# GpSimd writes the first two blocks' one-hots, and three more chunks are gathered raw

## What is computed

```
agg = segment_sum(layernorm(x)[src], dst)        # 106250 edges, 6250 nodes of 256 numbers
h   = relu(agg @ W_rel + b_rel + layernorm(x) @ W_root)
gates = h @ W_ih.T + b_ih + b_hh ; ... ; x = x + h_lstm @ W_fc + b_fc
x = x + ffn(layernorm(x))                        # slice softmax, attention over 64 slices per head
```

## Time and profile before

| | |
|---|---|
| median of 3 runs | 1261.83 us (1261.62 to 1261.88) |
| profiled execution, span | 1262.5 us |
| PE / PE weight load busy | 89% / 77% |
| DVE / ACT / POOL busy | 66% / 50% / 64% |

### The profile page before, as it was taken

How to read it: one execution, slowest core, us unless ns; L and a number is a source line. 1 busy time by engine, 2 the same in 40 slices (tenths; PEclk the granted TensorE clock), 3 DMA queues, 4 the chain that set the end, 5 groups by cost and what they waited for, 6 DMA issues and landing times. The chain is left out here.

```text
span 1262.5 us, 26644 instructions
## 1 busy us (share of the span) xinstructions
PE 1122.5 (89%) x9821; PEld 978.2 (77%) x9821; DVE 832.7 (66%) x2580; ACT 627.7 (50%) x1257; POOL 807.2 (64%) x850
## 2 busy tenths in 40 slices
PE   1058799999899999999999999999998999999998
PEld 1047688788788887888878787878787888897798
DVE  7885476567466765676667656775665667646665
ACT  5862344454455444544554545454543564545332
POOL 5277777777777777777777777777777777400000
PEclk9997999999899999999999999999998999999999
DMA  9573444444444444444444444444443444323398
GB/s 326 202 259 117 130 124 127 146 137 137 121 147 137 136 123 145 137 138 122 146 146 129 121 146 144 134 118 146 145 136 114 146 145 130 91 68 98 126 334 296
DMA packets 89761, 188.47 MB, mean 149 GB/s; under 512 B 19196, under 2 KB 51938, under 8 KB 89648
## 3 DMA queue, kind: packets, MB, share of 16 engines
q0 software_dynamic: 39888, 108.97, 29.9%
q1 hardware_dynamic: 38900, 57.91, 14.0%
q10 hardware_dynamic: 10859, 20.05, 4.5%
HBM read 154.86 MB, written 32.00 MB: 148 GB/s over the span
## 5 line engine op out<-in xcount | busy, mean ns | idle before, releaser
L618 POOL DMA_INDIRECT ring<-table,sidx x813 | 781.1, 961 | 271.6 <-issue 269.2
L397 PE MATMUL ps<-h_h,wih_h 128*128 128x250 f32 x1200 | 341.5, 285 | 0.0
L398 PE MATMUL ps<-h_l,wih_h 128*128 128x250 f32 x1200 | 338.8, 282 | 0.0
L399 PE MATMUL ps<-h_h,wih_l 128*128 128x250 f32 x1200 | 338.7, 282 | 0.0
L397 PEld LDWEIGHTS ps<-h_h,wih_h 128*128 128x128 f32 x1200 | 233.0, 194 | 1.6 <-issue 0.4
L398 PEld LDWEIGHTS ps<-h_l,wih_h 128*128 128x128 f32 x1200 | 232.8, 194 | 1.1
L399 PEld LDWEIGHTS ps<-h_h,wih_l 128*128 128x128 f32 x1200 | 232.5, 194 | 0.0
L983 PE MATMUL ps<-ring,oneh 128*32 128x512 f16 x2321 | 148.5, 386 | 55.1 <-DMA ring<-table,sidx 44.3
L762 ACT ACTIVATE gate<-ps,bgate 128x250 f32<-128x250 f32 x300 | 124.4, 468 | 143.1 <-PE ps L399 143.1
L1410 DVE TENSOR_SCALAR oneh<-iota,didx 128x64 f16<-128x64 f16 (+2 forms) x1199 | 183.2, 257 | 0.9 <-issue 0.9
L983 PEld LDWEIGHTS ps<-ring,oneh 128*32 128x32 f16 x2321 | 61.7, 97 | 125.0 <-DMA ring<-table,sidx 58.8
(11 more groups left out here) (211 smaller groups left out, 2480.1 us busy)
## 6 DMA issues: line engine op xcount, KB each, us to landing
ring<-table,sidx POOLq DMA_INDIRECT x813
swt_d<-swt ACTq DMA_DIRECT2D x25, 500.0 KB
gate<-swt_d SPq DMA_DIRECT2D x19, 500.0 KB, 5.9
x_room<-in_x SPq DMA_DIRECT2D x12, 512.0 KB, 10.2
xn<-table SPq DMA_DIRECT2D x25, 224.0 KB
xin<-in_x SPq DMA_DIRECT2D x25, 224.0 KB
res<-xin SPq DMA_DIRECT2D x25, 224.0 KB
table<-tile_room SPq DMA_DIRECT2D x8, 512.0 KB, 3.0
```

What stands on the lines that cost most here:

```text
L397: eng.matmul(dst, wh, xh, start=first, stop=False)
L398: eng.matmul(dst, wh, xl, start=False, stop=False)
L399: return eng.matmul(dst, wl, xh, start=False, stop=last)
L618: pool.indirect_dma_start(ring[:, j, :], None, table, bass.IndirectOffsetOnAxis(ap=idx, axis=0)).then_inc(done, 16)
```

## The change

1. POOL writes the one-hots of blocks 0 and 1 (`hots(pool, 0)`, `hots(pool, 1)`), after its raw gathers and before its wait for the stored table. DVE writes them only in the general branch; its turn 0 loses them.
2. `RAW` goes from 18 to 21, so `NE` from 6 to 7: 21 chunks are gathered raw and 810 from the table, and one more piece of three chunks is normalised in the ring.
3. The temporaries of all pieces lie in `norm_room`; the two lent table tiles begin at slot 21.
4. PE waits for all the raw pieces ahead of block 0's sums, where before it waited for each piece at its first use.

```diff
-    RAW = 18
+    RAW = 21
...
-        ln = [free[:, k * words:(k + 1) * words].rearrange("p (r c) -> p r c", c=C) for k in range(2)]
+        ln = [norm_room[:, k, :].rearrange("p (r c) -> p r c", c=C) for k in range(2)]
         tiles = [tile_room[:, k, :] for k in range(4)]
-        tiles += [free[:, (2 + k) * words:(3 + k) * words] for k in range(2)]
+        tiles += [free[:, k * words:(k + 1) * words] for k in range(2)]
...
-        e_ln = [norm_room[:, q, 0:3 * C].rearrange("p (r c) -> p r c", c=C) for q in range(2)]
 
         def ln_tmp(k):
-            return ln[k % 2] if k <= NCH else e_ln[k % 2]
+            return ln[k % 2][:, 0:ln_shape(k)[1], :]
...
+        def hots(eng, b):
+
+            e, (plan, _) = b % 2, hot_plan(b)
+            after(eng, sum_done[e], b // 2)
+            for j, (w0, w1, at) in plan.items():
+                n = WIN * (w1 - w0)
+                last = eng.tensor_scalar(oneh[:, e, at:at + n], iota[:, WIN * w0:WIN * w1], didx[:, j:j + 1],
+                                         -float(WN * b), ALU.subtract, ALU.is_equal)
+            last.then_inc(hot_done[e], 1)
...
             general = pool.value_load(flag_i[0:1, 0:1], min_val=0, max_val=1)
-            for q in range(TILES):
-                pool.wait_ge(ln_out[q], 16 * len(range(q, NCH + 1, TILES)))
-            pool.sem_inc(gather_go, 1)
+            pool.wait_ge(list_d, 2)
+
+            def table_stored():
+                for q in range(TILES):
+                    pool.wait_ge(ln_out[q], 16 * len(range(q, NCH + 1, TILES)))
+                pool.sem_inc(gather_go, 1)
...
             with pool.If(general):
+                table_stored()
...
+            with pool.Else():
+                hots(pool, 0)
+                hots(pool, 1)
+                table_stored()
...
                 pe.wait_ge(hot_done[e], b // 2 + 1)
+                if b == 0:
+                    for q in range(2):
+                        pe.wait_ge(ln_lo[q], len(range(q, NLN, 2)))
...
                             pe.wait_ge(rows_in[k % NGRP], 16 * GS * (k // NGRP + 1))
-                            if landed[0] < RAW:
-                                piece = NCH + 1 + k
-                                pe.wait_ge(ln_lo[piece % 2], piece // 2 + 1)
...
+                hots(dve, 0)
+                hots(dve, 1)
...
                 if isinstance(t, int) and t == 0:
-                    hots(0)
-                    hots(1)
                     add_halves(0, 0)
                     low_w1()
-                    hots(2)
+                    hots(dve, 2)
                     add_halves(0, 1)
```

More of the change, by code:

```diff
@@ L1592, in turn @@
                 if gather and gnn:
-                    hots(2 * t + 1)
+                    hots(dve, 2 * t + 1)
                 if gnn:
@@ L1603, in turn @@
                 if ahead:
-                    hots(2 * t + 2)
+                    hots(dve, 2 * t + 2)
                 if ffn:
```

## The result

The changed kernel takes 1266.65 us (median of 4, 1266.18 to 1268.17) beside 1261.86 us before: 0.4% slower, ratio 1.0041 with a 95% interval of 1.0029 to 1.0054. I had forecast 1258.6 us, 1256.4 to 1262.0. The profiled execution has a span of 1264.4 us in a time of 1266.18 us, so 1.8 us lie around the span here. The span of before in its profile, 1262.5 us, is longer than its median time less 1.8, so the profiled execution of before ran about 2.4 us longer than its middle timed one. So the two spans differ by 1.9 us only, where the medians differ by 4.8.

The account below looks back on a forecast made before the run. POOL's fixed-pace gather stream after its wait at chunk 36 was taken to bound the kernel. A 3.90 us gain less 0.7 on DVE gave 3.2 us, so 1261.83 - 3.2 = 1258.6 us, range 1256.4 to 1262.0.

Parts of the forecast that it names:

- What bounds the kernel: POOL's gathers at a fixed pace after its only wait, then PE's tail; moving that gather moves the end.
- T: POOL's issue of the table gather for chunk 36, at 88.33 us before; forecast 3.2 us earlier.
- Part 1, raw chunks: Three more raw gathers in POOL's idle time: POOL side of T falls to 82.53; extra piece costs 2.47 us.
- Part 2, PE's side of T: One-hots off DVE: PE begins block 0's sums at 78.8, T goes to 84.43, a gain of 3.90 us.
- the DVE term: Low halves on DVE delayed by POOL instructions: 0.7 us taken off the gain, range 0 to 1.7 us.
- Part 3, the price on POOL: 44 one-hots at 0.18 us plus 5.3 us of collisions end at 58.1 us, hidden before the stores end at 61.9.
- the 0.40 of my sum: Price in us of each one-hot on POOL at which all the forecast gain is gone.
- Part 4, the price on DVE: Six low halves on DVE each wait half a POOL instruction of 0.23 us, 0.7 us in all.
- Part 5: Temporaries in `norm_room` instead of the ring: no instruction added, costed at nothing.
- the one on the other side: POOL's one-hots too slow: at 0.5 us each, T 4.5 us later, 1266.3 us; chance 0.08.
- The burst that holds DVE: A low half waits for all POOL's one-hots: T slips by 4.0 us, 1265.8 us; chance 0.07.

Follow-up runs that it names:

- e1_block0_pool: Changed kernel with block 1's 24 one-hots back on DVE, POOL writing only block 0's 20; 1258.56 us, 0.9972 of the kernel before.
- e2_raw21_dve: Changed kernel with all one-hots back on DVE in turn 0, 21 raw chunks kept; 1263.96 us, 1.0013 of the kernel before.
- e3_raw18_pool: Changed kernel with 18 raw chunks instead of 21, POOL writing both blocks' one-hots; 1265.88 us, 1.0030 of the kernel before.
- e5_low_psum: Changed kernel with the low halves' second operand read from blank PSUM from the ninth piece on; 1260.17 us, 0.9993 of the kernel before.
- r_raw24: Changed kernel with block 1's one-hots on DVE, PE waiting piece by piece, 24 raw chunks; 1259.29 us, 0.9940 of the kernel before.
- e10_delay: Kernel before plus 14 spare one-hots of 32 columns on POOL in front of chunk 36; 1273.64 us, 1.0069 of the kernel before.

## Why the prediction was wrong, by its steps

- **What bounds the kernel**: right. The end goes with T: -4.0 and -3.3 us in e1_block0_pool, +2.4 and +2.1 in e2_raw21_dve, +4.1 and +4.1 in e3_raw18_pool, -1.9 and -1.7 in e5_low_psum, -7.3 and -7.6 in r_raw24, but +6.1 and +4.8 in the changed kernel. In all 13 lines of the table the shift of T lies within the interval of the time's shift, so one for one fits; 0.8 of it lies within 12 of the 13, so that is not excluded.
- **Part 1, raw chunks**: right. e2_raw21_dve has the 2.47 us. What I left out is that a raw gather beside a low half is lengthened here too: two of the three took 1.58 us instead of 0.95, and the one-hots began at 46.07 and not at 44.9.
- **Part 2, PE's side of T**: right. PE began at 79.52 where the sum with the DVE term says 79.5, and e1_block0_pool, where this side is the bound, has T at 84.38 for 84.4 to 85.1.
- **Part 3, the price on POOL**: this is the step that failed, by the size of one term. I took 0.18 us an instance, with 0.28 as the near upper bound. Undisturbed it is 0.48 on average, 21.08 us for 44. The row I went by, 0.23 us for 128 columns, writes only; the compare and fill of 0.28 us works on 4-byte numbers and takes no value per partition. Of the trace's rows neither does what these instructions do, and I let nearness in width and type stand for nearness in work. I also called the gather the only kind with which POOL reads SBUF; the compare and fill reads its tile `ident` too. The collisions were 7.6 us for my 5.3, and the nearness of the two numbers is partly luck. In the stretch that I had summed they cost 3.6 us, since an instance was held for less than the whole low half. The other 3.9 us come from five low halves of the raw pieces, which the instructions met because they lasted longer. So in place of the 58.1 us that I had for the end of the one-hots, start, price and collisions as measured give 46.1 + 21.1 + 7.6 = 74.8; the trace has 74.7. The stores were done by 62.2, so POOL's own work and not the table set the first gather, and T went to 94.41 instead of 85.1. As an estimate from these terms, T would have stayed at 88.33 with 0.34 us an instance, not with the 0.40 of my sum.
- **Part 4, the price on DVE**: right in sign, too large. Two low halves took 1.38 and 1.33 us instead of 1.22; the stores ended 0.3 us later, 0.17 of which this execution had at 38 us already. The last low half, which is what PE waits for, began at 78.31 instead of 77.74, so 0.4 us of it are left without that 0.17. I had taken 0.7.
- **Part 5**: nothing was seen of it; no run has the other room alone.
- **The rivals**: the one on the other side is what happened. At 0.5 us an instance it gave 1266.3 us; measured were 1266.65. That the time fits so well is partly luck: its T was 92.8 and came at 94.41, while the median rose by only 4.8 us. I gave it 0.08. The far end of the price that I had named, 1.25 us, lay beyond the break-even of 0.40, so nothing in the trace excluded this case, and 0.08 was too small a chance for it. The range, which I had closed at 1262.0, left it out. The burst that holds DVE did not show: no low half was lengthened by more than 0.15 us.

The rule of the Trainium skill ("SBUF — State Buffer", section "Who interferes with whom") on two SBUF inputs of DVE against a GpSimd instruction that reads SBUF is borne out by e5_low_psum: 7.6 us with the second input in SBUF, and none of the nine long ones with it in PSUM. In the other direction two low halves became 0.15 and 0.10 us longer. That the later one is blocked does not fit every pair: three of the nine instances on POOL began 0.08 to 0.10 us before the low half beside them, and they were the ones that became longer, while the low half kept its 0.94 us.

## What to carry to other kernels

In this kernel the engine that sets the pace has room only before its stream begins, and that room is a number: 16.6 us between the last raw gather and the stored table in e2_raw21_dve. Work moved into it is worth what its own instructions cost on that engine, so bound that from rows that read, compute and write as it does, and where there are none take the break-even price (0.40 us by my sum, about 0.34 by the measured terms) as the question to be measured, not as a side case. Moving 20 of the 44 one-hots fitted and gained 0.3 to 0.4%; moving all lost 0.4%.

## What the runs showed of the hardware

- A two-operation TENSOR_SCALAR on POOL, f16 in and out with one value per partition, took 0.27 us and 3.4 ns a column (0.38, 0.49, 0.60 us at 32, 64, 96 columns); with one operation it took 0.27 us and 2.5 ns a column (0.35, 0.43, 0.51 us). On DVE 44 of them took 6.64 us one behind the other, 0.15 us each; on POOL undisturbed 21.08 us, 3.2 times as much.
- In the changed kernel nine of them overlapped a DVE instruction with two inputs in SBUF and took 1.03 to 1.61 us; they ended 0.25 to 0.47 us after it. In e10_delay two in a row took 1.29 and 1.26 us beside four such instructions in a row. With DVE's second input in PSUM (e5_low_psum) none of this was seen.
- The busy time of the indirect gathers differed between two executions of one kernel, on two chips, by up to 0.8%: 760.4 and 766.4 us for the same 795. That is enough to hide or feign a change of this size in a single profile.
